# Cross-attention values in 32-column tiles, the pair split later, cross queries earlier in the step

## The reference, cut to what matters

```python
x = _layernorm(x + _L0_attn_ref(x, w_q, w_k, w_v, w_o))
x = _layernorm(x + _L0_xattn_ref(x, ctx, ctx, mask, Wq, bq, Wk, bk, Wv, bv, Wo, bo))
x = _layernorm(x + _L0_ffn_ref(x, router_w0, wg0, wu0, wd0, router_w1, wg1, wu1, wd1))

# in _L0_xattn_ref, H = 16 heads of DK = 16
scores = jnp.einsum('bhqd,bhkd->bhqk', qh, kh) / np.sqrt(DK)
scores = jnp.where(mask[:, None, :, :] == 0, NEG, scores)
attn = jax.nn.softmax(scores, axis=-1)
out = jnp.einsum('bhqk,bhkd->bhqd', attn, vh)     # the product whose tiles change
...
# in _moe_group: route, sort by expert, gate/up/down, add back by weight
expert_weights, expert_indices = lax.top_k(scores, top_k)
```

## Time and profile before

| | |
|---|---|
| median of 3 runs | 4668.85 us (4668.39 to 4672.15) |
| the profiled execution | 4678.94 us, its span 4677.2 us |
| PE (TensorE matmul) busy | 4486.3 us, 96% |
| PEld (weight load) busy | 3939.7 us, 84% |
| DVE (VectorE) busy | 3684.6 us, 79% |
| ACT (ScalarE) busy | 3298.4 us, 71% |
| POOL (GpSimd) busy | 2689.0 us, 57% |
| first phase | up to about 3641 us |
| second phase, first matmul | 3676.68 us |

### The profile page before, as it was taken

One profiled execution on the slowest core, in us unless ns is written; L12 is line 12 of the kernel. 1 busy time (PEld: TensorE's weight loads), 2 busy tenths in 40 slices (PEclk: granted clock), 3 DMA queues, 4 the chain that ended last, 5 costly groups with the idle time before them and its releaser, 6 DMA issues. The chain is left out here.

```text
span 4677.2 us, 129797 instructions
## 1 busy us (share of the span) xinstructions
PE 4486.3 (96%) x38848; PEld 3939.7 (84%) x38848; DVE 3684.6 (79%) x18057; ACT 3298.4 (71%) x12741; POOL 2689.0 (57%) x3747
## 2 busy tenths in 40 slices
PE   7999999999999999999999999999997699999998
PEld 7888888888888888888888888888886587888876
DVE  4788888888888888888888888888887366657888
ACT  5777787877778777787877877777776244444444
POOL 3355555555555555555555555555555555557777
PEclk9999999999999999999999999999999799999999
DMA  4111111111121111111121111111114399998999
GB/s 163 54 63 62 63 64 65 63 61 62 63 68 63 61 62 66 63 63 63 60 69 62 63 63 60 67 62 62 62 59 155 112 325 356 317 308 264 309 306 291
DMA packets 477422, 552.08 MB, mean 118 GB/s; under 512 B 55633, under 2 KB 408145, under 8 KB 476241
## 3 DMA queue, kind: packets, MB, share of 16 engines
q1 hardware_dynamic: 350800, 296.21, 19.6%
q0 software_dynamic: 52224, 146.87, 8.3%
q10 hardware_dynamic: 73728, 100.70, 7.0%
HBM read 266.21 MB, written 277.35 MB: 116 GB/s over the span
## 5 line engine op out<-in xcount | busy, mean ns | idle before, releaser
L898 ACT ACTIVATE prob<-prob,negmax 128x128 f32<-128x128 f32 x2048 | 796.5, 391 | 298.9 <-DVE negmax L1032 298.9
L1032 DVE CUSTOM_DVE_ANT_0 prob<-bank,causal 128x128 f32<-128x128 f32 x2048 | 453.4, 286 | 508.4 <-PE bank L787 403.8
L898 ACT ACTIVATE xprob<-xprob,xnegmax 128x128 f32<-128x128 f32 x2048 | 797.8, 397 | 3.5 <-DVE xnegmax L1032 3.5
L1363 POOL DMA_INDIRECT y_d<-y,to x576 | 563.8, 979 | 351.4 <-DVE y L1505 328.6
L634 POOL DMA_INDIRECT xs_d<-xrow,place x512 | 521.2, 1018 | 385.2 <-DMA xs_d<-blank 248.0
L1416 PE MATMUL bank<-moe,xgT 128*128 x2304 | 595.7, 381 | 0.1
L597 POOL TENSOR_TENSOR rs<-spread_v,minus_half 128x1 f32<-128x1 f32 x256 | 170.9, 667 | 628.6 <-DVE spread_v L1106 628.6
L685 PE MATMUL bank<-xT0h,wqkv 128*128 128x256 f32 x2048 | 441.0, 299 | 20.5 <-DVE wqkv L434 11.8
L1032 DVE CUSTOM_DVE_ANT_0 xprob<-bank,xmask 128x128 f32<-128x128 f32 x2048 | 451.7, 286 | 3.3 <-PE bank L787 1.7
L1069 DVE TENSOR_TENSOR prob<-prob,inv 128x512 f32<-128x512 f32 x512 | 440.1, 860 | 17.5
L685 PE MATMUL bank<-xT1h,wqkv 128*128 128x256 f32 x2048 | 436.1, 296 | 0.0
(11 more groups left out here) (174 smaller groups left out, 13497.1 us busy)
## 6 DMA issues: line engine op xcount, KB each, us to landing
xg<-xs_d SPq DMA_DIRECT2D x576, 129.0 KB
xs_d<-blank SPq DMA_DIRECT2D x248, 272.0 KB
rows<-y_d ACTq DMA_DIRECT2D x256, 256.0 KB
xT_s<-xT SPq DMA_DIRECT2D x128, 128.0 KB, 2.6
cT<-cT SPq DMA_DIRECT2D x128, 128.0 KB, 2.0
x_s<-x SPq DMA_DIRECT2D x128, 128.0 KB, 2.4
x_d<-x SPq DMA_DIRECT2D x128, 128.0 KB, 1.9
sums<-x_d ACTq DMA_DIRECT2D x128, 128.0 KB
```

Of the source, the lines that this page charges most:

```text
L898: last = nc.scalar.activation(dst[:, h, :], dst[:, h, :], ACT.Exp, bias=src_bias[:, h:h + 1], scale=-1.0, accum_out=acc[:, h:h + 1])
L1032: last = nc.vector.tensor_tensor_reduce(dst[:, h, :], heads(h), bias[:, :], -1.0, float("inf"), ALU.add, ALU.min, least[:, h:h + 1])
L1363: nc.gpsimd.indirect_dma_start(y_d[:, :], bass.IndirectOffsetOnAxis(ap=to[:, m % NTO:m % NTO + 1].bitcast(U32), axis=0), y_s[q][:, :], Non ...
```

## The change

It has four parts.

1. Cross values: `cross_mix` now makes 8 products of 32 columns, two heads wide, in four column tiles; two products add up in each quarter of the result. `xvD` shrinks from 4 x 320 to 8 x 96 elements per partition (1280 to 768), and the write into it follows.
2. VectorE, even step: the move of the cross queries goes ahead of x2, and the mask and the cross values go ahead of `weigh` and `cross_normalise`.
3. VectorE, odd step: the high half of the split goes from between the two `normalise` to behind `rank_moves`.
4. GpSimd and ScalarE: the scatter of slots 0 and 1 goes from distance 13 to 14 (odd to even), that of slots 2 and 3 from 14 to 15 (even to odd), `token_rows` and `owners` from 10 to 11 (even to odd), `root(0)` goes behind the scatter, and `x_low` goes to the end of the step.

```diff
-            xvD = [sb(f"xvD{p}", [P, KC * 2, XHALF * (4 * XD + XD)]) for p in (0, 1)]
+            xvD = [sb(f"xvD{p}", [P, KC * 4, 2 * (2 * XD + XD)]) for p in (0, 1)]
...
@@ GpSimd, double_step
                         b = due(n, 14, NB)
                         if b is not None:
-                            scatter(b, (2, 3))
+                            scatter(b, (0, 1))
                         b = due(n, 12, NB)
                         if b is not None:
                             open_blocks(b)
-                        if split_pair(n) is not None:
-                            x_low(split_pair(n))
                         b = due(n, 8, NB)
                         if b is not None:
                             root(1, b)
-                        b = due(n, 3, NB)
-                        if b is not None:
-                            root(0, b)
-                        b = due(n, 13, NB)
-                        if b is not None:
-                            scatter(b, (0, 1))
...
+                        b = due(n, 15, NB)
+                        if b is not None:
+                            scatter(b, (2, 3))
+                        b = due(n, 3, NB)
+                        if b is not None:
+                            root(0, b)
+                        b = due(n, 11, NB)
                         if b is not None:
                             token_rows(b)
+                        if split_pair(n) is not None:
+                            x_low(split_pair(n))
@@ TensorE, cross_mix
-                        for j in range(XHALF):
-                            for side in (0, 1):
-                                last = nc.tensor.matmul(jb(n, "xy")[HALVES[side], 0:P], xvD[b % 2][:, 2 * c + side, j * 4 * XD:(j + 1) * 4 * XD],
-                                                        xprobT[:, side * PH + j, :], start=(j == 0), stop=(j == XHALF - 1))
+                        for j in (0, 1):
+                            for r in range(4):
+                                last = nc.tensor.matmul(jb(n, "xy")[r * ROWS:(r + 1) * ROWS, 0:P], xvD[b % 2][:, 4 * c + r, j * 2 * XD:(j + 1) * 2 * XD],
+                                                        xprobT[:, 2 * r + j, :], start=(j == 0), stop=(j == 1))
@@ ScalarE, owners
-                        b = due(n, 10, NB)
+                        b = due(n, 11, NB)
@@ VectorE, even_step
+                        b = job_of(n, "xq")
+                        if b is not None:
+                            dve.wait_ge(made["xq"], b + 1)
...
                         if b2 is not None:
                             dve.wait_ge(rsqrt_ready[1], b2 + 1)
@@ VectorE, odd_step
                         normalise(n, 0)
-                        if split_pair(n) is not None:
-                            wait(dve, made["v1"], 2 * split_pair(n) - 2)
-                            x_split_high(split_pair(n))
                         normalise(n, 1)
...
                         rank_moves(n)
+                        if split_pair(n) is not None:
+                            wait(dve, made["v1"], 2 * split_pair(n) - 2)
+                            x_split_high(split_pair(n))
                         cross_normalise(n, 0)
```

More of the change, by code:

```diff
@@ L1001, in double_step @@
                             move_v(n, "v1")
-                            owners(n)
                         else:
@@ L1010, in double_step @@
                             move_v(n, "v0")
+                            owners(n)
                     steps_of(double_step)
@@ L1190, in even_step @@
                         normalise(n, 1)
-                        if b2 is not None:
-                            dve.wait_ge(rsqrt_ready[1], b2 + 1)
-                            wait(dve, x2_out[b2 % 2], b2 // 2 * 16)
-                            wait(dve, xrow_ready, b2 - 1)
-                            nc.vector.tensor_scalar(x2[b2 % 2][:, :], sum2[:, :], mv[:, 1, 0:1], rs[:, 1:2],
-                                                    ALU.subtract, ALU.mult).then_inc(x2_ready, 1)
-                        weigh(n)
-                        cross_normalise(n, 0)
                         b = job_of(n, "xq")
@@ L1205, in even_step @@
                             last.then_inc(moved["xq"], 1)
+                        if b2 is not None:
+                            dve.wait_ge(rsqrt_ready[1], b2 + 1)
+                            wait(dve, x2_out[b2 % 2], b2 // 2 * 16)
+                            wait(dve, xrow_ready, b2 - 1)
+                            nc.vector.tensor_scalar(x2[b2 % 2][:, :], sum2[:, :], mv[:, 1, 0:1], rs[:, 1:2],
+                                                    ALU.subtract, ALU.mult).then_inc(x2_ready, 1)
+                        if b is not None:
                             dve.wait_ge(mask_in, (b + 1) * 16)
@@ L1209, in even_step @@
                             nc.vector.tensor_tensor(
-                                xvD[b % 2][:, :, :].rearrange("p h (j d) -> p h j d", j=XHALF)[:, :, :, 0:XD],
-                                jb(n, "xv")[:, 0:D].rearrange("p (h j d) -> p h j d", h=2 * KC, j=XHALF),
-                                xbv_s[:, :].rearrange("p (h j d) -> p h j d", h=2 * KC, j=XHALF), ALU.add).then_inc(moved["xv"], 1)
+                                xvD[b % 2][:, :, :].rearrange("p h (j d) -> p h j d", j=2)[:, :, :, 0:XD],
+                                jb(n, "xv")[:, 0:D].rearrange("p (h j d) -> p h j d", h=4 * KC, j=2),
+                                xbv_s[:, :].rearrange("p (h j d) -> p h j d", h=4 * KC, j=2), ALU.add).then_inc(moved["xv"], 1)
+                        weigh(n)
+                        cross_normalise(n, 0)
                     def odd_step(n):
```

## The result

The changed kernel takes **4516.18 us** (median; 4514.94 to 4519.07), beside 4670.50 for the kernel before (the median of four executions of it now): ratio **0.9669**, 95% interval 0.9653 to 0.9686. It is 3.3% faster; 4512 was forecast.

What follows compares the result with a forecast made beforehand. TensorE, busy 98% at full clock, was taken to bound the first phase; 4678.94 - 75 (cross values) - 82 (stalls) = 4522 us profiled, 10 us lower as median: 4512. Its own range was 4490 to 4535, the full range 4475 to 4590.

Steps and rivals of the forecast that it cites:

- Part 1, size: Cross values on PE, line 846: four groups instead of eight pairs save 0.30 us net per call, 250 calls, 75 us.
- Two at a time: Rival at line 846: only two quarters run together, eight groups remain plus the entry, 30 us lost, 4617 us; chance 0.10.
- loads shown: Rival at line 846: each quarter group shows its weight load, saving only 0.14 us per call, 35 us, 4552; chance 0.08.
- one after another: Rival at line 846: the quarters run singly, costing 1.0 us per call, 250 us, 4837 us, slower than before; chance 0.03.
- Parts 2 and 3, the stalls: PE's waits at `rank` and the cross scores go once split and queries move: 82 us, bounds 60 and 91.
- That stall goes in all ordinary steps: PE's cross scores no longer wait for the cross queries, written 1.8 us ahead of the next step: 22 us.
- I cost these at nothing: Moved scatters, `owners` and smaller clear of `xvD` cost nothing; 2 us if the first phase's tail stretches by one scatter.
- runs late on POOL and then on DVE: Even step behind a split, kernel before: cross queries end 1.57 us into the odd step, which then takes 14.93 us.
- The sum of parts: Whole kernel: savings of 75 and 82 us, each priced against the kernel before, were subtracted together from 4678.94.
- The new wait: Rival: late split, or DVE waiting for xq, costs 0.5 us in every split step, 31 us, 4543 us; chance 0.14.
- so 1.0 us remains: DVE's even step: despite 0.55 us new idle time, it still ends 1.0 us before its next masked scores.
- The tail: End of the first phase: no saving forecast; 2 us of loss if it stretches by one scatter.

Runs made afterwards that it cites:

- tiles with scatters: The kernel before with only the 32-column cross-value tiles and the new order of scatters, `x_low` kept in front of `root(1)`: 4620.67 us, ratio 0.9843.
- the late split alone: The kernel before with only the split moved to the end of the odd step, `x_low` last on POOL behind the scatters: 4802.04 us, ratio 1.0262.

## Why the prediction was right, and where it was not

**The total and the bound: right.** 4512 against 4516.18. The forecast for the profiled execution was 4522 and it took 4515.24; the 10 us by which before's profiled run lay above its median did not recur. Two small errors nearly cancel, so the 4 us between the two medians say little about the single terms.

**Part 1, size: right.** 0.30 us per call, from terms that all measured as priced: group to group 0.11, entry 0.20, second group 0.13 (0.11 + 0.02 against 0.11 + 0.03). "Two at a time", "loads shown" and "one after another" are out: four tiles start within 0.03 us, and the loads of 0.11 us each lie under the running matmuls. The rule of the Trainium skill, "TensorE: Matmul & The Clock Gate", Part 3, by which a weight load overlaps only if the row group differs, does not hold for these column tiles.

**Parts 2 and 3, the stalls: right in size and for `rank`.** The late split keeps `rank`'s wait away (measured by undoing it: 68 us in all, forecast 54). Its cover was larger than feared: `x_low` ended 0.47 us into the next step, forecast 0.9, and the masked scores had 0.95 us to spare, forecast 0.5.

**"That stall goes in all ordinary steps": right as a row, but its cause is not the one priced.** The wait at the cross scores is gone. In the kernel before, either part takes it out of the ordinary steps by itself: the order of the queries (14.39 us in the mean, from 14.74), or part 4 (49 of 60 steps at about 14.4). In the changed kernel part 4 does it: undone alone, the order of the queries costs 4 us, not 22. There it only chooses at which product PE meets a late DVE.

**"I cost these at nothing" (part 4): the step that failed.** Moving two scatters from the end of the odd step to its front was said to be free, since POOL is busy only 57%. PE shows no wait from the new place, but the sentence stopped there: it never asked what the place left behind was worth. Without part 4 the change as a whole gains nothing (1.0015). In the old place the first scatter of slots 0 and 1 wants `place` of the same step and cleared rows, and POOL idles 2.1 us for them in nearly every odd step, with all its later work behind. One step later it waits for neither. POOL's idle time in front of scatters, before (280 to 3540 us) and after (280 to 3400 us; the 0.3 between two scatters and the like):

```profile
POOL xs_d L634 <- DMA xs_d<-blank: 241.6, 115, 2.4
...
POOL xs_d L634 <- issue: 120.3, 470, 2.1
```

The sign of the lateness stood in the prediction itself: the even step behind a split "runs late on POOL and then on DVE", with POOL's last scatter at 1179.04. I took this for a result of the split alone.

**The sum of parts: wrong as a method.** The four parts alone measure +92, -13, +122 and -11 us on 4670, together +190; jointly they give -155. The prediction priced each against the kernel before and added, as if PE's 0.30 us per call stayed PE's. A shorter row on the bound engine takes 0.30 us of cover from every chain beside it in each step. (Cover is the time by which a chain is done before PE needs its result.) The total came out because part 4 had restored that cover, not because the terms are independent; that part 4 was in the change, priced at nothing, was luck for the forecast.

**The new wait (a rival at 0.14): it did come, at about half of its price (17 us, priced at 31) and elsewhere.** It was placed at the masked scores of the step behind a late split. What happened is one step later. The cover of the even step ("so 1.0 us remains") was worked out for the step from 1150.40, which has no split in front of it. Behind a split the last division takes 1.69 beside `yTl`, and DVE ends 2.7 us into the odd step. That takes 0.27 us in every second odd step, 17 us in all.

**The tail: 12 us not forecast**, most of it by part 4, for which the prediction feared 2 us of loss.

Not separated: how much of part 4 is the scatters and how much `token_rows` and `owners`, which moved with them; and why a few single steps of 16 to 20 us remain where a part of the late chain is left (six in the kernel before, three in tiles with scatters).

## What to carry to other kernels

Before a row of the bound engine is shortened, list the spare time of the chains that run beside it, in the step where it is least and not in an ordinary one; the saving is real only up to that. Price a moved instruction at both ends: what it meets in the new place, and what its old place gives back (here, 2.1 us of waiting of GpSimd in each odd step). Single parts tried alone would have condemned two of the four here, so a change whose parts lend each other cover is to be judged whole, and then by undoing one part at a time.

## What the runs showed of the hardware

- **A long idle time can cost twice.** Waits of 2.1 and 2.3 us on PE were followed by a granted clock of 0.50 (1.2 GHz) for 2 to 3 us of full work, and a wait of 2.26 us cost 3.8. Not every one was: between 280 and 3400 us the late split alone has 54 waits of 1.7 to 2.2 us with 47 such falls, and the kernel before five of 1.9 to 2.1 us with three. The two kernels with 107 and 110 waits of up to 0.9 us kept 1.00 over the stretch.
- **VectorE beside GpSimd.** A division of two 128x512 operands takes 0.69 us alone, and 1.58 to 1.80 where it lies beside a large `TENSOR_TENSOR` of POOL in the rows above; `hot`, 0.28, becomes 1.12 beside the rows of tokens. The Trainium skill, "GPSIMD Engine Reference", section 8, says that the two share their SBUF interfaces and contend when VectorE reads two SBUF inputs or runs in a 2-port mode; the trace agrees for the division, with 0.9 to 1.1 us more per meeting. Operations with one input were lengthened too: after the change the cast of the experts' numbers (line 1155) takes 0.90 us beside the rows of tokens, 0.16 before. Which mode it runs in no run shows.
- **Column tiles of 32 in float32 run four at a time**, with starts 7 ns apart and groups 0.11 us apart, the same spacing as two tiles of 64.
